# Four of the eight direct dbx units of a Mamba loop made by scaled transposes in place of a spreading matmul

## What is computed

```
def _mamba_layer(x, in_w, cw, cb, xp_w, dtw, dtb, A_log, D, ow):
    xz = jnp.einsum('bld,ed->ble', x, in_w)
    xi, z = jnp.split(xz, 2, axis=-1)
    ...
    dt, Bm, Cm = jnp.split(dbc, [DT_RANK, DT_RANK + D_STATE], axis=-1)
    delta = jax.nn.softplus(jnp.einsum('blr,dr->bld', dt, dtw) + dtb)
    y = _selective_scan(xc, delta, -jnp.exp(A_log), Bm, Cm, D)
    y = y * jax.nn.silu(z)
    return jnp.einsum('bld,od->blo', y, ow)

# _selective_scan, for each token:
h = dA * h + (d_t * u_t)[:, :, None] * b_t[:, None, :]   # dA = exp(d_t A)
y = jnp.einsum('bds,bs->bd', h, c_t)
```

## Time and profile before

| | us |
|---|---|
| median of 3 runs (1530.0 to 1530.98) | 1530.02 |
| the profiled execution, whole | 1532.95 |
| its span in the trace | 1530.7 |
| steps of the Mamba loop in the trace, `zs` of the first to `zs` of the last | 694.1 to 1456.48 |

### The profile page before, as it was taken

One profiled execution on the slowest core, in us unless ns is written; L12 is line 12 of the kernel. 1 busy time (PEld: TensorE's weight loads), 2 busy tenths in 40 slices (PEclk: granted clock), 3 DMA queues, 4 the chain that ended last, 5 costly groups with the idle time before them and its releaser, 6 DMA issues. The chain is left out here.

```text
span 1530.7 us, 21758 instructions
## 1 busy us (share of the span) xinstructions
PE 1255.4 (82%) x6427; PEld 620.1 (41%) x6427; DVE 1146.2 (75%) x1605; ACT 1045.8 (68%) x1804; POOL 965.2 (63%) x918
## 2 busy tenths in 40 slices
PE   6454689898836999977798998999899998999884
PEld 3341334343323547633343444444444444444331
DVE  7754468677786321238899999999999999999985
ACT  4323579788834122347588899888898889888871
POOL 5642311010185540058799898988998899989893
PEclk9775789899965999989899999999999999999988
DMA  2112232122214402330342344224341434234301
GB/s 59 42 46 98 89 97 84 65 89 72 86 30 160 132 21 66 114 84 24 83 104 71 77 95 97 71 71 108 85 98 55 99 87 106 59 73 95 93 8 55
DMA packets 84321, 120.47 MB, mean 79 GB/s; under 512 B 17410, under 2 KB 43256, under 8 KB 83848
## 3 DMA queue, kind: packets, MB, share of 16 engines
q1 hardware_dynamic: 77294, 100.60, 25.0%
q0 software_dynamic: 6816, 18.42, 4.0%
q10 hardware_dynamic: 122, 0.39, 0.1%
HBM read 96.15 MB, written 24.77 MB: 79 GB/s over the span
## 5 line engine op out<-in xcount | busy, mean ns | idle before, releaser
L2168 DVE TENSOR_TENSOR_SCAN hs<-decay,dbx 128x512 f32<-128x512 f32 x512 | 591.6, 1204 | 44.0 <-ACT decay L2050 20.4
L1746 POOL TENSOR_TENSOR hcm<-hs,Cc 128x1024 f32<-128x1024 f32 x192 | 452.9, 2367 | 24.6 <-DVE hs L2168 16.4
L2050 ACT ACTIVATE decay<-dtr,a_cur 128x512 f32<-128x512 f32 x512 | 350.7, 710 | 2.2 <-DVE hs L2168 1.9
L1870 PEld LDWEIGHTS dbx<-ident_sb,scaled 128*128 128x128 f32 x1536 | 178.5, 143 | 284.2 <-issue 126.7
L1870 PE MATMUL dbx<-ident_sb,scaled 128*128 128x128 f32 x1536 | 245.2, 284 | 52.8 <-POOL scaled L1729 27.3
L2028 ACT ACTIVATE scaled<-duT,BT 128x256 f32<-128x256 f32 x506 | 224.6, 496 | 27.4 <-PE dbx L1870 26.8
L1739 POOL TENSOR_TENSOR hck<-hs,Cc 128x512 f32<-128x512 f32 x128 | 163.3, 1276 | 54.5 <-DVE hs L2168 50.6
L1867 PE MATMUL dbx<-du,spread_sb 128*128 128x512 f32 x256 | 146.6, 656 | 12.5 <-DVE hs L2168 12.5
L883 ACT ACTIVATE ex<-tt 128x1024 f32<-128x1024 f32 x128 | 136.9, 1070 | 4.4 <-DVE tt L968 3.7
L1797 PE MATMUL slots<-XT,w_tap 128*128 128x512 f32 (+1 forms) x240 | 124.4, 606 | 3.8 <-PEq L1242 3.8
L1729 POOL TENSOR_SCALAR scaled<-duT,BT 128x256 f32<-128x256 f32 x256 | 118.3, 480 | 0.0
(11 more groups left out here) (331 smaller groups left out, 2026.5 us busy)
## 6 DMA issues: line engine op xcount, KB each, us to landing
dtr<-dt_turn SPq DMA_DIRECT2D x60, 512.0 KB, 7.7
Cc<-bc_turn SPq DMA_DIRECT2D x256, 64.0 KB, 2.1
dt_turn<-dt SPq DMA_DIRECT2D x15, 512.0 KB, 2.8
Bb<-bc_turn SPq DMA_DIRECT2D x64, 64.0 KB, 2.0
conv_row<-in_conv_row SPq DMA_DIRECT2D x4, 512.0 KB, 5.8
w_rg<-in_w_rg SPq DMA_DIRECT2D x8, 256.0 KB, 2.7
w_ru<-in_w_ru SPq DMA_DIRECT2D x8, 256.0 KB, 3.1
w_rd<-in_w_rd SPq DMA_DIRECT2D x8, 256.0 KB, 3.8
```

What stands on the lines that cost most here:

```text
L1746: nc.gpsimd.tensor_tensor(hcm[:, (m - 1) % MR:m % MR + 1, :], hs[:, q % HR:p % HR + 1:p - q, :], Cc[:, k:k + 1, :].broadcast_to([P, 2, 512 ...
L1870: last = nc.tensor.transpose(dbx[bank_of[p]][:, P * kk:P * kk + P], scaled[:, (b + k) % 2, kk, g, :, :].rearrange("p j c -> p (j c)"), ide ...
L2050: nc.scalar.activation(dec[:, p % DR, :], dtr[:, b % 2, g, :], ACT.Exp, scale=a_cur[:, 4 * g + k:4 * g + k + 1]).then_inc(s_dec, 1)
L2168: nc.vector.tensor_tensor_scan(hs[:, p % HR, :], dec[:, p % DR, :], dbx[bank_of[p]][:, :], 0.0, ALU.mult, ALU.add).then_inc(s_sc, 1)
```

## The change

The direct units g = 0 to 3 (p = 3, 7, 11, 15; `TURNED` = 4) get their dbx as the others do: four transposes of a new buffer `scaled3`, and no `times_b`. The direct units g = 4 to 7 stay as they are. `scaled3` is filled by 16 scalings of 128x128 values for each step: eight on ScalarE (after w = 24 to 27 one each, after w = 30 and 31 two each) and eight on GpSimd (after p = 22 to 29 one each), for the next step. For the first step they are issued inside it, on ScalarE after w = 0 and 1, on GpSimd ahead of p = 0. `duT` is now a single buffer, and its copy waits for all scalings of the step before.

```diff
-            DIRECT = 3
+            DIRECT, TURNED = 3, 4
...
+            scaled3 = sb(st5, "scaled3", [P, 4, TURNED, 4, 32])
...
-            duT = sb(st5, "duT", [P, 2, 4, 256])
+            duT = sb(st5, "duT", [P, 4, 256])
...
+                    def scale_turned(l, n, x):
+                        j, kk = x % 4, x // 4
+                        if x == 8:
+                            wait(pool, s_bx, at(l, n - 1, UN, place[DIRECT, TURNED - 1] + 1))
+                            pool.wait_ge(s_bt, at(l, n, 1, 1))
+                            pool.wait_ge(s_dut, at(l, n, 1, 1))
+                        nc.gpsimd.tensor_scalar(scaled3[:, kk, :, j, :], duT[:, kk, 0:32 * TURNED].rearrange("p (g c) -> p g c", c=32),
+                                                BT[:, n % 2, kk, 4 * DIRECT + j:4 * DIRECT + j + 1], 1.0, ALU.mult, ALU.mult).then_inc(s_k[DIRECT], 1)
...
                         for p in range(UN):
+                            if first(l, b) and p == 0:
+                                for x in range(8, 16):
+                                    scale_turned(l, b, x)
                             if units[p][0] == DIRECT or units[p][1] % 2 == 1:
                                 weigh(l, b, p)
+                            if 22 <= p < 30 and more(l, b + 1):
+                                scale_turned(l, b + 1, p - 14)
...
                         if g == 0:
-                            if k == DIRECT:
-                                pe.wait_ge(s_dun, at(l, b, 2, 2))
-                            else:
-                                pe.wait_ge(s_k[k], at(l, b, 16, 16))
+                            pe.wait_ge(s_k[k], at(l, b, 16, 16))
...
-                        if k == DIRECT:
+                        if k == DIRECT and g >= TURNED:
+                            if g == TURNED:
+                                pe.wait_ge(s_dun, at(l, b, 2, 2))
                             mm(dbx[bank_of[p]][:, :], spread[:, g % 4, :], du[:, b % 2, g // 4, :], start=True, stop=True).then_inc(s_bx, 1)
                         else:
+                            src = scaled3[:, :, :, :, :] if k == DIRECT else scaled[:, (b + k) % 2, :, :, :, :]
                             for kk in range(4):
-                                last = nc.tensor.transpose(dbx[bank_of[p]][:, P * kk:P * kk + P], scaled[:, (b + k) % 2, kk, g, :, :].rearrange("p j c -> p (j c)"), ident[:, :])
+                                last = nc.tensor.transpose(dbx[bank_of[p]][:, P * kk:P * kk + P], src[:, kk, g, :, :].rearrange("p j c -> p (j c)"), ident[:, :])
...
                     def copy_dut(l, n):
-                        wait(act, s_k[1], at(l, n - 1, 16, 0))
+                        for k in range(4):
+                            wait(act, s_k[k], at(l, n, 16, 0))
...
+                    turned_scales = {24: (0,), 25: (1,), 26: (2,), 27: (3,), 30: (4, 5), 31: (6, 7)}
...
-                            if u % 4 == 3:
+                            if u % 4 == 3 and u // 4 >= TURNED:
                                 times_b(l, b, u // 4)
```

More of the change, by code:

```diff
@@ L1576, in build_stages @@
             s_dt, s_dtc, s_dun, s_yv = map(sem, ("dt_in_psum_ready", "dt_copied", "du_ready", "yv_ready"))
-            s_k = [sem(f"scaled_by_b{k}") for k in range(3)]
+            s_k = [sem(f"scaled_by_b{k}") for k in range(4)]
             s_bx, s_mul, s_dec, s_sc, s_hc, s_ys, s_fm, s_fk = map(sem, ("dbx_in_psum", "dbx_times_b", "decay_ready", "scan_done", "hc_ready", "y_started", "hcm_folded", "hck_folded"))
@@ L1728, in scale_by_b @@
                             pool.sem_inc(s_turn, 1)
-                        nc.gpsimd.tensor_scalar(scaled[:, (n + 1) % 2, kk, :, j, :], duT[:, n % 2, kk, :].rearrange("p (g c) -> p g c", c=32),
+                        nc.gpsimd.tensor_scalar(scaled[:, (n + 1) % 2, kk, :, j, :], duT[:, kk, :].rearrange("p (g c) -> p g c", c=32),
                                                 BT[:, n % 2, kk, 4 + j:5 + j], 1.0, ALU.mult, ALU.mult).then_inc(s_k[1], 1)
+                    def scale_turned(l, n, x):
[6 more added lines that the diff above has]
+                                                BT[:, n % 2, kk, 4 * DIRECT + j:4 * DIRECT + j + 1], 1.0, ALU.mult, ALU.mult).then_inc(s_k[DIRECT], 1)
                     def weigh(l, b, p):
@@ L1769, in _ @@
                             for x in range(10, 16):
-                                nc.gpsimd.tensor_scalar(scaled[:, 0, x // 4, :, x % 4, :], duT[:, 0, x // 4, :].rearrange("p (g c) -> p g c", c=32),
+                                nc.gpsimd.tensor_scalar(scaled[:, 0, x // 4, :, x % 4, :], duT[:, x // 4, :].rearrange("p (g c) -> p g c", c=32),
                                                         BT[:, 0, x // 4, x % 4:x % 4 + 1], 1.0, ALU.mult, ALU.mult).then_inc(s_k[0], 1)
@@ L2027, in scale_by_b, with scale_turned @@
                                 act.wait_ge(s_bx, at(l, n, UN, last_of(0) + 1))
-                        nc.scalar.activation(scaled[:, (n + k) % 2, kk, :, j, :], duT[:, n % 2, kk, :].rearrange("p (g c) -> p g c", c=32),
+                        nc.scalar.activation(scaled[:, (n + k) % 2, kk, :, j, :], duT[:, kk, :].rearrange("p (g c) -> p g c", c=32),
                                              ACT.Copy, scale=BT[:, n % 2, kk, 4 * k + j:4 * k + j + 1]).then_inc(s_k[k], 1)
+                    def scale_turned(l, n, x):
+                        j, kk = x % 4, x // 4
+                        if x == 0:
+                            wait(act, s_bx, at(l, n - 1, UN, place[DIRECT, TURNED - 1] + 1))
+                            act.wait_ge(s_bt, at(l, n, 1, 1))
+                            act.wait_ge(s_dut, at(l, n, 1, 1))
+                        nc.scalar.activation(scaled3[:, kk, :, j, :], duT[:, kk, 0:32 * TURNED].rearrange("p (g c) -> p g c", c=32),
+                                             ACT.Copy, scale=BT[:, n % 2, kk, 4 * DIRECT + j:4 * DIRECT + j + 1]).then_inc(s_k[DIRECT], 1)
                     def d_of_layer(l):
@@ L2057, in step @@
                             decay(l, b, w)
+                            if first(l, b) and w < 2:
+                                for x in range(4 * w, 4 * w + 4):
+                                    scale_turned(l, b, x)
                             if w == 0 and not first(l, b):
@@ L2082, in step @@
                                         scale_by_b(l, n, 0, x)
+                                if w in turned_scales:
+                                    for x in turned_scales[w]:
+                                        scale_turned(l, n, x)
                             if w == 18 and not first(l, b):
@@ L2154, in times_b @@
                         p = place[DIRECT, g]
-                        if g == 0:
+                        if g == TURNED:
                             dve.wait_ge(s_c3[b % 2], by_parity(l, b, 128))
@@ L2162, in scan @@
                         dve.wait_ge(s_dec, at(l, b, UN, p + 1))
-                        if k == DIRECT:
-                            dve.wait_ge(s_mul, at(l, b, 8, g + 1))
+                        if k == DIRECT and g >= TURNED:
+                            dve.wait_ge(s_mul, at(l, b, 8 - TURNED, g - TURNED + 1))
                         else:
```

3 lines of the change are left out of this document (2 added, 1 removed).

## The result

The changed kernel takes 1546.81 us (median of 4 runs, 1544.23 to 1551.43), the kernel before 1530.01 (4 runs). The ratio is 1.0115, with a 95% interval of 1.0089 to 1.0142: slower by 16.8 us, where 11.4 was forecast; it lies in the range of 1532 to 1557. The profiled execution took 1547.41, its span is 1545.6.

A forecast was written before the change was run, and what follows sets the result against it. A ring of waits through TensorE and GpSimd, ScalarE on a side branch with 0.72 us slack, was taken as the bound; 12.1 + 1.0 - 1.7 = +11.4 us on the median 1530.02 gave 1541.4, range 1532 to 1557.

The forecast's parts named there:

- The ring's turn over ScalarE: Mamba step: the TensorE-GpSimd cycle of waits would run over ScalarE, whose 2.45 us of scalings exceed 0.72 slack.
- The size of a steady step: Mamba loop: +1.73 from late `z`, -0.95 from TensorE's transposes, so +0.78 us a step; +1.17 at a layer's start.
- The clock: Rival: TensorE's clock falls behind the new wait ahead of `z`, costing 24 us, to 1565; chance 0.12.
- the wait of 0.95: TensorE, ahead of the fold of v = 19: 0.95 us, to grow to about 2; such waits don't lower the clock.
- the sum: Whole kernel: 12.1 for 14 steps, +1.0 for the first, -1.7 for the last, together +11.4 us.
- What lies behind a wait, counted at 0: Steady steps: turned units p = 11 and 15, where TensorE waits anyway, and VectorE's relief would each save 0.
- VectorE's saving: Four `times_b` a step removed relieve VectorE of 3.0 us, which becomes idle time: 0 in steady steps.
- GpSimd at 0: GpSimd, p = 22 to 29: eight scalings, about 2.5 us a step, fit its idle time and cost 0.
- the whole delay of `z` (1.73): TensorE's `z`: ScalarE's 2.45 us of scalings less 0.72 of slack start it 1.73 us later.
- the +1.0 of GpSimd: First step: eight GpSimd scalings, 2.5 us, exceed 1.45 idle and delay the gathers behind them by 1.0 us.
- the -1.7 of the last step: Last step: one `times_b` (0.76) and a half-clock matmul traded for transposes (0.97) save 1.7 us.
- the unknown price of a scaling: ScalarE, 128x128: 0.306 us taken, bounds 0.20 and 0.41, giving ends of 1529.5 and 1553.

The follow-up runs named there:

- e3: Kernel before (direct units by matmul, with `times_b`) plus only ScalarE's eight scalings, their result unread, none on GpSimd: 1554.81 us, ratio 1.0176.
- e2: Changed kernel without ScalarE's eight scalings, TensorE waiting for GpSimd's eight alone: 1527.21 us, ratio 0.9999 to the kernel before.
- e1: Changed kernel with ScalarE's eight scalings moved ahead of its wait for unit 20: 1530.98 us, ratio 1.0016 to the kernel before.
- e5: Changed kernel without GpSimd's eight scalings, ScalarE's kept: 1582.64 us on another chip, ratio 1.0142 to the kernel before.
- e11: Changed kernel with four ScalarE scalings ahead of its wait for unit 20, four behind `silu_xi`, no added matmuls: 1525.64 us, ratio 0.9986 to the kernel before.
- e4: Changed kernel plus two matmuls of constants on TensorE ahead of the wait for the fold of v = 19: 1539.03 us, ratio 1.0069 to the kernel before.
- e6: e1 plus the two added matmuls of e4: 1563.89 us on another chip, ratio 1.0004 to the kernel before.
- e10: e11 plus the two added matmuls of e4: 1512.64 us, ratio 0.9903 to the kernel before.
- e12: Changed kernel with 16 transposes where e4 has two added matmuls: 1542.68 us, ratio 1.0102 to the kernel before.
- e7: e1 with only p = 3 and 7 turned, p = 11 and 15 again by matmul and `times_b`: 1565.88 us on another chip, ratio 1.0015 to the kernel before.
- e8: Kernel before with `times_b` of g = 0 to 3 left out, nothing else changed: 1561.05 us on another chip, ratio 0.9999.

## Why the prediction was right, and where it was off

**The ring's turn over ScalarE: right.** The stretch of 17.6 (17.53), the wait of 1.6 to 1.8 ahead of `z` (1.6; 1.85 at a layer's start), the scaling of 394 ns (388) came as forecast. e3 shows the cost alone, e2 its removal.

**The size of a steady step: 0.90 for 0.78.** The scalings were 0.29 apart, not 0.306, so the stretch grew by 2.32 instead of 2.45. But `z` starts 0.15 behind the end of `silu_xi` (1167.61 against 1166.20 + 1.26), where I let it start at once; and from the start of `z` to the fold of v = 8 it went from 1070.89 - 1057.58 = 13.31 to 12.44, so 0.87 instead of 0.95, since `z` after a wait takes 1.10 instead of 1.02. 2.32 - 0.72 + 0.15 - 0.87 = 0.88, and 0.90 was measured. At a layer's start it is 50.90 - 49.73 = 1.17, as predicted.

**The clock: right idea, wrong place.** I looked for a fall behind the new wait ahead of `z`. It came behind an old wait that the change made longer. I had written that the wait of 0.95 would grow to about 2 and that the waits of 0.95 don't make the clock fall, and I didn't put the two together. Over the changed kernel, e1, e2, e5 and e11, 35 of 39 waits of about 2.2 ahead of this fold were followed by half clock, and none of 31 of about 1.6. But all those 31 lie in steps whose clock had fallen behind v = 10 already, and none of the 39 does, so these alone don't tell a short wait from a fall just past. The steps without an earlier fall do: of their waits of about 0.5 (e4, e6, e10, e12) none of 29 was followed by half clock, of those of 0.92 to 0.98 (before, e3, e7) none of 22, of those of 1.8 (e8) one of nine. This missed term is 6.3 of the 18.8 us (five falls); the sum had 10 x 0.78 + 3 x 1.17 = 11.3 for these 13 intervals, so it accounts for most of the 7.5 that it lacked there.

The prediction named a rule of the Trainium skill (TensorE: Matmul & The Clock Gate, Part 4: PE-mode transpose), by which transposes don't count as busy for the clock gate in the way that matmuls do. e12 doesn't agree: with 16 transposes ahead of the wait the clock stayed up in all six steps that had not had a fall already, as it did with two matmuls in all seven such steps of e4. The measurement decides; here the length of the wait told.

**What lies behind a wait, counted at 0: not nothing.** This goes for the turned units of p = 11 and 15 and for VectorE's `times_b`. Together they relieve ScalarE's wait for the output projection and make the wait ahead of the fold long enough for the falls (e7). By itself VectorE's saving takes no time off a step, as predicted, but in the steps without an earlier fall it makes 0.85 us of that longer wait (e8), and so has a part in the missed term.

**GpSimd at 0: right** (e5). Its eight scalings take 2.80 us in the first step, 0.35 each for the 0.31 that was estimated, and fit all the same.

**The first interval.** Of what the prediction counted, it holds the whole delay of `z` (1.73) and the +1.0 of GpSimd, and no saving yet, since that comes behind `z`: 2.73, measured +4.96. e4, which has the same scalings and the same late `z`, has +1.76; e1 and e10, which have the same scalings on GpSimd and no late `z`, have -0.04 and -0.08. That is the delay of `z` and nothing for the +1.0. The 3.2 by which the changed kernel exceeds e4 go with VectorE's slow instructions (last section), not with the added scalings.

**The last interval and the end.** The last interval has the saving and no late `z` at its end, -0.95; with the -1.7 of the last step that makes -2.65, measured -1.63 and -1.57, together -3.20. That the -1.57 is near -1.7 shows little: what follows the last `zs` was 74.22 before and wanders from 72.48 (e2) to 76.19 (e6) in the others. The last interval is 2.0 to 2.1 shorter than before in e2, e10 and e11 and only 0.58 in e1; what makes it more than 0.95 stays open. e8, without `times_b` alone, has 0.15 less in it.

**The stages ahead of the loop** took 5.7 us less in the profiled execution, with no cause in the change that I could name. So it is luck that its total, +14.5, looks close to the sum of 11.4, for the loop and its end lost 20.6. That the median lies in the range is owed in part to a range made wide by the unknown price of a scaling, which itself was well met.

## What to carry to other kernels

Ask of each instruction added which wait it stands behind: the same eight scalings cost 1.85 us a step behind the last wait ahead of a hand-over, and nothing where four are ahead of it and four fill a wait of their own engine (steps of 48.81 in e10, 48.82 without them in e2). When an engine is relieved, look at the wait it comes to earlier: made longer, it can bring the clock down behind it, and the saving is gone; filling matmuls ahead of it were worth 11.7 us here (e10 against e11). Work that lies where its engine waits anyway is not thereby worth nothing: see what other engines take from behind it. VectorE's saved 3 us took nothing off a step of e8, and yet made TensorE's wait 0.85 longer.

## What the runs showed of the hardware that was not expected

In the first step, VectorE mixes the experts' rows in with an instruction that takes 0.347 us in the median. A few of the 32 take far longer. The instructions of that line in the changed kernel and in e10, durations in ns (min/median/max):

```profile
L2182 DVE SCALAR_TENSOR_TENSOR GATE<-dtr,share,GATE x32: 339/347/8390, 683.9 to 734.0; 128x128 f32<-128x128 f32 x32
```

```profile
L2187 DVE SCALAR_TENSOR_TENSOR GATE<-dtr,share,GATE x32: 339/347/4857, 683.3 to 731.1; 128x128 f32<-128x128 f32 x32
```

The longest is 4.62 to 4.86 in the kernel before, e1, e3, e4, e5, e8 and e10, and 8.39 in the changed kernel, 8.41 in e11, 8.45 in e12, 9.69 in e2, 9.80 in e6 and 9.86 in e7. The first interval goes with it: 66.0 to 68.3 in the first seven, 69.3 to 71.1 in the others. e1, e6, e10 and e11 have the same scalings in this step, and two of them are in either group. Most of the extra time lies in one group of eight of these instructions, which takes 4.50 to 4.83 in the first seven kernels and 10.35 to 11.82 in the others. VectorE's timeline of it in the changed kernel and in e1:

```profile
698.72 10.35 DVE L2182 SCALAR_TENSOR_TENSOR GATE<-dtr,share,GATE 128x128 f32<-128x128 f32 x8
```

```profile
699.80 4.71 DVE L2182 SCALAR_TENSOR_TENSOR GATE<-dtr,share,GATE 128x128 f32<-128x128 f32 x8
```

The 5.6 us between them are more than the 5.0 by which the first intervals differ (71.08 and 66.08). In the changed kernel GpSimd runs products and scalings without a gap over most of that time; whether that holds VectorE up was not tested.

What a fall of the clock costs hangs on where it lies. Each of the 14 steps of the changed kernel has exactly one; the nine behind v = 10 are free, the five behind the fold cost 1.1 to 1.35 us. The same place isn't free in every kernel: a fall behind v = 10 costs 0.3 us in e7 (49.93 against 49.61), 0.6 in e6 (49.86 against 49.25) and under 0.1 in e10; why e6 and e10 differ is open.
